# Layer 1: the four expert rows that ScalarE weights are added up on GpSimd instead of VectorE

## The reference

```
x = x + L0_attn(layernorm(x), ctx)
x = x + L0_ffn(layernorm(x))     # 64 experts, the 8 best of each row, weights normalised
x = x + L1_attn(layernorm(x), ctx)
x = x + L1_ffn(layernorm(x))
```

```
top_w, top_idx = top_k(softmax(x @ W_router), 8)
top_w = top_w / sum(top_w)
out[t] = x[t] + sum over k of top_w[t, k] * expert(top_idx[t, k])(x[t])
```

## Time and profile before

| | us |
|---|---|
| median of 3 executions | 2049.42 (2048.53 to 2051.22) |
| profiled execution, span from first to last instruction | 2053.3 |
| VectorE busy in the whole span | 1414.6 (69%) |
| TensorE busy | 1665.0 (81%) |
| ScalarE busy | 1265.1 (62%) |
| GpSimd busy | 983.7 (48%) |

### The profile page before, as it was taken

One profiled execution on the slowest core, in us unless ns is written; L12 is line 12 of the kernel. 1 busy time (PEld: TensorE's weight loads), 2 busy tenths in 40 slices (PEclk: granted clock), 3 DMA queues, 4 the chain that ended last, 5 costly groups with the idle time before them and its releaser, 6 DMA issues. The chain is left out here.

```text
span 2053.3 us, 45004 instructions
## 1 busy us (share of the span) xinstructions
PE 1665.0 (81%) x12724; PEld 1127.2 (55%) x12879; DVE 1414.6 (69%) x4335; ACT 1265.1 (62%) x3302; POOL 983.7 (48%) x1114
## 2 busy tenths in 40 slices
PE   3999899999984999999998278888888888755551
PEld 1555555555543888888997134444444444444440
DVE  5888888888864455455433479999999999743331
ACT  1777677777761566666665268888888887721210
POOL 4367677777764000000000666666666662148883
PEclk9999999999996999999999589999999999979996
DMA  5689877777747976666665668888777775178856
GB/s 140 158 209 246 217 209 217 211 213 215 205 132 233 288 224 196 196 200 195 203 199 174 165 175 211 226 222 205 197 193 201 194 195 145 51 191 187 175 94 112
DMA packets 413088, 390.98 MB, mean 190 GB/s; under 512 B 46640, under 2 KB 385072, under 8 KB 412848
## 3 DMA queue, kind: packets, MB, share of 16 engines
q1 hardware_dynamic: 346496, 265.28, 48.8%
q0 software_dynamic: 37904, 90.22, 17.0%
q10 hardware_dynamic: 28448, 32.59, 5.5%
HBM read 233.74 MB, written 170.16 MB: 197 GB/s over the span
## 5 line engine op out<-in xcount | busy, mean ns | idle before, releaser
L1114 DVE TENSOR_REDUCE mx<-psS 128x2 f32<-128x512 f32 x1024 | 679.3, 675 | 100.4 <-PE psS L1507 66.8
L911 ACT ACTIVATE prob<-psE 128x512 f32<-128x512 f32 x1024 | 600.8, 594 | 226.0 <-PE psE L1520 209.2
L760 POOL DMA_INDIRECT yg<-y_d,row_all x256 | 248.7, 971 | 632.2 <-SPq L406 480.7
L1520 PE MATMUL psE<-q,k 128*128 128x256 bf16 x2048 | 394.7, 275 | 38.1 <-issue 15.9
L1507 PE MATMUL psS<-k,q 128*128 128x512 bf16 x869 | 336.5, 389 | 22.4 <-DMA k<-k_stack_d 12.8
L1630 PE MATMUL psE<-wt,xgT 128*128 (+1 forms) x1536 | 324.7, 335 | 2.0 <-ACT xgT L1010 1.6
L1459 DVE TENSOR_TENSOR hid<-sil,psE 128x96 f32<-128x96 f32 x384 | 97.8, 255 | 330.0 <-ACT sil L1015 329.8
L747 POOL DMA_INDIRECT xs_d<-xr,row_all x256 | 252.1, 985 | 111.0 <-ACT prob L911 67.6
L1520 PEld LDWEIGHTS psE<-q,k 128*128 128x128 bf16 x2048 | 185.6, 98 | 193.8 <-ACT prob L911 75.0
L1536 PE MATMUL psO<-prob,v 128*32 128x256 f32 x4096 | 275.9, 387 | 9.0 <-ACT osb L891 9.0
L1010 ACT COPY xgT<-psS 128x256 f32<-128x256 f32 x384 | 144.5, 376 | 187.1 <-PE psS L1624 170.2
(11 more groups left out here) (220 smaller groups left out, 2639.9 us busy)
## 6 DMA issues: line engine op xcount, KB each, us to landing
xg<-xs_d SPq DMA_DIRECT2D x320, 128.0 KB, 2.6
y_d<-y_all SPq DMA_DIRECT2D x320, 128.0 KB, 2.3
q<-q_stack_d SPq DMA_DIRECT2D x128, 256.0 KB
k<-k_stack_d SPq DMA_DIRECT2D x128, 256.0 KB
wt<-in_gu ACTq DMA_DIRECT2D x110, 192.0 KB, 3.3
q_stack_d<-parts SPq DMA_DIRECT2D x64, 192.0 KB
k_stack_d<-parts SPq DMA_DIRECT2D x64, 192.0 KB
wt<-in_dn ACTq DMA_DIRECT2D x110, 96.0 KB, 3.9
```

The costliest lines, as they stand in the source:

```text
L760: g.indirect_dma_start(yg[:, k, :], None, y0_d[:, :], bass.IndirectOffsetOnAxis(row_all[:, row(st.pair("load") * K + k, 1)], 0))\
L911: a.activation(prob[gr][:, u % 4, :], psE[ring][:, :], ACT.Exp, scale=SCALE).then_inc(s_exp, 1)
L1114: v_.tensor_reduce(mx[b][:, bg // 4, :].rearrange("p (h r) -> p h r", h=2)[:, :, (bg % 4) * 2 + tt], psS[(UNITS * (st.s0 - LAG["smax"]) + ...
L1520: ins = m_.matmul(psE[ring][:, i * T:(i + 1) * T], k2[b][:, bg, hh * T + i * P:hh * T + (i + 1) * P], q2[b][:, bg, :], start=True, stop=True)
```

## The change

In steps 6 to 32 TWO and ONE leave VectorE. GpSimd does both, in place and with the same shapes: the 128x512 addition between its second and third gather, where it waits for the four products of ScalarE (s_comb), and the 128x256 addition between the fourth and fifth gather. A new semaphore s_half tells VectorE that both are done; ALL waits for it. VectorE's own rows 6 and 7 move one unit forward, from units 7 and 8 to 6 and 7. The steps before step 6 keep the old form.

```diff
-ADDED, TWO, ONE, ALL, MOMENTS = (4, 5, 7, 8), 6, 7, 9, (10, 11)
+ADDED, ALL, MOMENTS = (4, 5, 6, 7), 9, (10, 11)
+HALVED = (2, 4)
...
     if s0 >= FULL:
-        return ADDED, TWO, ONE, ALL, MOMENTS
+        return ADDED, None, None, ALL, MOMENTS
...
+                def halves(n):
+                    if not st.on("comb"):
+                        return
+                    done = 2 * (st.s0 - FULL)
+                    if n == 2:
+                        pool.wait_ge(s_comb, st.n1("comb", 4))
+                    else:
+                        pool.wait_ge(s_half, done + 1)
+                    g.tensor_tensor(ys[:, 0:n, :], ys[:, 0:n, :], ys[:, n:2 * n, :], ALU.add).then_inc(s_half, 1)
...
                     if st.s0 >= FULL:
                         for k in range(K):
+                            if k in HALVED:
+                                halves(2 - HALVED.index(k))
                             gather(st, k, PACE[L][k])
...
                     if u == all_:
-                        ch.join("one")
+                        if st.s0 >= FULL:
+                            dve.wait_ge(s_half, 2 * (st.s0 - FULL + 1))
+                        else:
+                            ch.join("one")
```

More of the change, by code:

```diff
@@ L388, in build @@
         s_eq, s_hote = sem("s_eq"), sem("s_hote")
-        s_sum, s_match = sem("s_sum"), sem("s_match")
+        s_sum, s_match, s_half = sem("s_sum"), sem("s_match"), sem("s_half")
         s_chain = sem("s_chain")
```

## The result

| | before | after |
|---|---|---|
| median, us | 2048.98 (2046.48 to 2051.22, 4 runs) | 2092.27 (2084.50 to 2097.19, 4 runs) |
| ratio after to before | | 1.0206, 95% interval 1.0188 to 1.0223 |
| profiled execution, span | 2053.3 | 2095.5 |
| one full step of layer 1's attention | 19.08 | 20.53 |

The change makes the kernel 2% slower, by 43.3 us. The forecast was 2060.9 us with a range up to 2068. Its direction and its mechanism (GpSimd's additions hold up VectorE's operations with two SBUF inputs, on the part of VectorE's line that sets the step) hold. Its size is wrong by nearly a factor of four: 43.3 us longer instead of 11.5.

A forecast was written before the change was run, and what follows sets the result against it. A ring through VectorE, TensorE and ScalarE bounds the step: 0.74 blocked - 0.20 - 0.10 = 0.44 us, x 24 = 10.6, plus 0.9 for three early steps, on 2049.4 gives 2060.9 us; own range 2057 to 2065, 8-in-10 range 2050 to 2068.

The forecast's parts named there:

- The ring: Loop through VectorE, TensorE and ScalarE sets the step; without blocking, the change saves 0.30 us, giving 18.78 us.
- The wait before reduction 8: VectorE's wait for TensorE's scores before reducing unit 8 grows from 0.55 us by 0.33 to 0.88 us.
- The additions' own durations: On GpSimd the 128x512 addition takes 1.26 us and the 128x256 one 0.73 us, together 1.99 us.
- The addition runs from about 1441.21 to 1442.47 ... Blocked to 0.15 us before 1442.47, ranks starts at 1442.32: GpSimd's first addition blocks VectorE's ranks, due at 1441.57, making it 0.75 us late.
- the term of 0.74 us: Delay of VectorE's line per step from GpSimd's first addition, taken as 0.74 us.
- "No cost" for the second addition: GpSimd's second addition meets VectorE's row of unit 7; up to 0.73 us falls into the wait before reduction 8.
- I cost both at nothing: GpSimd's later remainder, awaited by ScalarE's cast, and VectorE's ALL waiting for s_half: both zero cost.
- the 1.03 us of room: Slack of some 1.03 us on GpSimd before gather 7, read from one full step, absorbing part of the additions' time.
- The third rival: GpSimd's second addition or later third part also holds a VectorE row, another 0.3 us a step: 2069 us, chance 0.10.

The follow-up runs named there:

- e5: The changed kernel without GpSimd's two additions and VectorE's wait for them, the sum leaving out expert rows 1 to 3: 2041.92 us beside 2048.69 before.
- e6: The changed kernel with a one-column GpSimd write ahead of each addition, whose end the addition waits for: 2072.97 us beside 2048.69 for the kernel before.
- e7: The changed kernel with GpSimd memsets of similar length instead of its additions, expert rows 1 to 3 left out: 2053.92 us beside 2047.73 before.
- e12: The kernel before with TWO moved from VectorE's unit 6 to 7 and ONE from 7 to 8, nothing on GpSimd: 2041.5 us, ratio 0.9957.
- e8: The changed kernel with both GpSimd additions one behind the other between the fifth and sixth gather: 2061.22 us, ratio 1.0064 to the kernel before.

## Why the prediction was wrong

**The ring: right.** Removal alone gives 18.78 us a step (e5), the number forecast. The wait before reduction 8 is 0.88 us, as said; it is the same with the blocking (after) and without (e5), so that it came true does not speak for the size of the blocking.

**The additions' own durations: right, with one addition.** 1.27 us against 1.26; the second takes 0.73 to 0.74 us where nothing meets it (0.73 forecast), and 0.96 where a row of VectorE is under way.

**"The addition runs from about 1441.21 to 1442.47 ... Blocked to 0.15 us before 1442.47, ranks starts at 1442.32": this step failed, twice.** First, the place. I had the addition 1.52 us behind the reduction of unit 4; it is 1.22 us behind (1458.24 less 1457.02). I reckoned GpSimd 0.10 us later against VectorE. ScalarE's products did come that much later, but the first gather now follows the third product by 0.36 us (e5, and after); before it was 0.65 us. Why is open. Second, and this decides, the port is taken about half a microsecond before the recorded start. In the 26 steps of the changed kernel in which the 128x512 addition stands behind a gather, every VectorE operation with two SBUF inputs that began between 0.58 and 0.25 us ahead of it was held to its end: the row of unit 4 in most, ranks or exm (128x16 and 128x64) in some. Those that began 0.73 us ahead or more went through. With the right place and the lock at the recorded start the row of unit 4 would just have slipped by (it would end at 1458.23), ranks would have been held about 0.46 us, and the loss would have been still smaller than forecast; e6 shows nearly that. So the term of 0.74 us, what the first addition blocks in each step, should have been 1.57, and the operation held is the row of unit 4, not ranks.

**"No cost" for the second addition: wrong by 0.16 us a step.** It too reaches ahead, and catches the end of the row of unit 6, which is on the path, not the row of unit 7.

The Trainium skill (SBUF — State Buffer, section "Who interferes with whom") has whoever issues first keep the shared ports for the whole instruction. By the records it is the other way in the changed kernel: VectorE's row started 0.48 us before the addition and was the one that waited. The rule fits only if "first" means the moment at which GpSimd's instruction is taken up, which no row shows; where GpSimd's operation was not queued (1147.36 above) the records agree with it, and the later one, GpSimd's, was held. Its statement that two SBUF inputs contend with GpSimd's reads alone agrees with e7: memsets held nothing up.

**"I cost both at nothing", for GpSimd's 2 us: right in the undisturbed steps, wrong over the whole.** e7 has 18.78 us a step with that time on GpSimd, and loses 9.9 us to e5 elsewhere. I judged the room from one full step. The row that would have warned me is GpSimd's gather with 3.00 us of idle time, twice in the kernel before: there the 1.03 us of room is gone already. Nor did the sum have TensorE's clock, which fell to 0.50 in these places after TensorE had waited.

The third rival (the port costs more than the first addition) comes nearest, 2069 us, and had a tenth of the chance. The sum lacked that bound: an operation of 0.47 us can be held for the whole addition and its lead, 1.57 to 1.72 us here, and I asked only which two operations lie inside the addition, not which lie just ahead of it.

## What to carry to other kernels

Before moving work to a second engine, find the ring or line that sets the step and ask what part of that work is on it: here 0.30 of 1.1 us. The same 0.3 us came from moving two sums in VectorE's own order (e12), without anything on another engine. When an operation goes to GpSimd, check every VectorE operation with two SBUF inputs not only during it but, if it stands behind a gather, from 0.6 us ahead, do the same for GpSimd's later operations that it pushes back, bound the price by the full length of the GpSimd operation, and judge GpSimd's room in its worst step, not in a typical one.

## What the runs showed of the hardware

- A 128x512 addition on GpSimd queued behind a gather holds up VectorE from up to 0.61 us before its recorded start (e8), for its whole length. With a one-column memset and a semaphore wait between them a row 0.49 us ahead passes (e6), and so does one 0.12 us ahead of an operation before which GpSimd idled (before). A row 0.04 us ahead of such an operation is held (e6, 1148.93: 1.48 us). GpSimd's remainder, where it stands right behind a gather, does the same as the addition: a 128x512 sum on VectorE 0.32 us ahead of it took 2.05 us instead of 0.68 (e12, 1201.34). For rows that begin less than about 0.6 us ahead of a queued operation the record of starts alone misleads on who holds whom.
- The held operation ends 0.29 us after the addition's end if it is a row of 0.47 us (after), so it seems to run its last 0.47 us from 0.18 us before that end; before the change it was 0.19.
- Of a 128x256 addition the row ahead of it is held much less (0.16 us) and the addition is lengthened, from 0.73 to 0.96 us. Begun 0.58 us ahead (after, 1398.19), it is held 0.50 us; in both cases it ends 0.58 us before the addition does. Why the two shapes differ is open.
- TensorE's granted clock was 0.50 in eight stretches of 3.4 us in the last 24 steps of the changed kernel, and in none of the kernel before; the two looked at follow on 2.38 and 2.69 us of idling of TensorE. Undisturbed steps, in which TensorE waits as long (2.42 us before 1462.70), kept 1.00. What decides between them is open.
- GpSimd idles 3.00 us before the same two gathers, 14 steps apart, in all 14 traces.
- One chip ran the kernel before in 2160.59 us, the others in 2047.73 to 2050.02 us.
